# Local attention of a two-layer transformer: the first tile's norms in front of the last stage's end, inverse norms in front of divisions, queries and keys turned next to each other

## The reference

```python
x = x + band_attention(layernorm(x), ctx, ctx)       # |i - j| <= 128
y = layernorm(x)
for l in range(2):
    h = shift_token(y)                               # the upper half of the columns comes from the row before
    q, k, v = split(h @ wqkv[l])                     # 8 heads of 64
    q, k = l2norm(q) * qs[l], l2norm(k) * ks[l]      # divided by the norm of each head's 64 elements
    q, k = rotary_xpos(q, k)                         # q*cos*scale + rotate_half(q)*sin*scale; k with 1/scale
    o = local_attention(q, k, v)                     # i - 256 <= j <= i, softmax
    y = y + o @ wo[l]
    h = layernorm(shift_token(y)) * g[l] + b[l]
    a, gate = split(h @ w1[l] + b1[l])
    y = y + (a * gelu(gate)) @ w2[l] + b2[l]
return x + y
```

## Time and profile before

| | |
|---|---|
| median of three runs | 3010.24 us |
| the profiled execution: its own time / its span | 3010.82 us / 3008.8 us |
| TensorE busy | 2960.5 us, 98% of the span |
| VectorE, ScalarE, GpSimd busy | 54%, 41%, 38% |
| mean granted TensorE clock | 0.996 |
| DMA | 63 GB/s mean |

### The profile page before, as it was taken

How to read it: one execution, slowest core, us unless ns; L and a number is a source line. 1 busy time by engine, 2 the same in 40 slices (tenths; PEclk the granted TensorE clock), 3 DMA queues, 4 the chain that set the end, 5 groups by cost and what they waited for, 6 DMA issues and landing times. The chain is left out here.

```text
span 3008.8 us, 44260 instructions
## 1 busy us (share of the span) xinstructions
PE 2960.5 (98%) x17040; PEld 2418.5 (80%) x17040; DVE 1613.9 (54%) x3359; ACT 1236.6 (41%) x2497; POOL 1138.1 (38%) x1202
## 2 busy tenths in 40 slices
PE   7999999999999999999999999999999999999999
PEld 6887888888878888888887888888878888888887
DVE  6975667766764333333324667776675333433331
ACT  5874555555564111111123655555565211111111
POOL 6756556655641101111103655665561111211111
PEclk9999999999999999999999999999999999999999
DMA  7651111111042111001122111111124111111110
GB/s 238 209 177 60 43 47 43 57 43 54 29 121 63 40 45 45 31 21 39 45 85 69 32 43 50 47 50 43 54 62 128 58 45 31 53 55 52 47 53 29
DMA packets 144181, 190.52 MB, mean 63 GB/s; under 512 B 21334, under 2 KB 75098, under 8 KB 143972
## 3 DMA queue, kind: packets, MB, share of 16 engines
q1 hardware_dynamic: 143972, 187.70, 19.6%
HBM read 132.44 MB, written 52.46 MB: 61 GB/s over the span
## 5 line engine op out<-in xcount | busy, mean ns | idle before, releaser
L991 PE MATMUL quad<-fhT_f,w_h_f 128*128 128x512 f32 (+1 forms) x1392 | 551.0, 396 | 1.5 <-ACT w_h_f L1055 1.5
L993 PE MATMUL quad<-fhT_f,w_l_f 128*128 128x512 f32 (+1 forms) x1392 | 544.9, 391 | 0.0
L992 PE MATMUL quad<-fhT_f,w_h_f 128*128 128x512 f32 (+1 forms) x1392 | 543.4, 390 | 0.0
L1650 DVE SCALAR_TENSOR_TENSOR u_f<-quad,bias_f,gate_f_raw 128x512 f32<-128x512 f32 (+1 forms) x174 | 130.4, 749 | 696.3 <-PE quad L993 613.4
L1719 POOL TENSOR_SCALAR stats<-stats 128x1 f32<-128x1 f32 x64 | 43.5, 680 | 1021.5 <-DVE stats L1625 1020.9
L1807 POOL TENSOR_TENSOR turned_qk<-with_cos,with_sin 128x256 f32<-128x256 f32 x256 | 188.7, 758 | 452.3 <-DVE with_cos L1534 360.6
L1210 ACT ACTIVATE lprob<-lprob,small 128x384 f32<-128x384 f32 (+2 forms) x512 | 288.5, 565 | 160.5 <-DVE small L1509 160.5
L1313 ACT ACTIVATE gate_f_raw<-quad,bias_f 128x512 f32<-128x512 f32 (+1 forms) x174 | 119.5, 687 | 507.0 <-PE quad L993 507.0
L1055 ACT ACTIVATE uT_f<-u_f 128x512 fp32r<-128x512 f32 (+2 forms) x176 | 117.3, 666 | 511.1 <-DVE u_f L1650 511.1
L761 PE MATMUL bank_pair<-wqkv_h,hT 128*128 128x512 f32 x992 | 320.2, 404 | 1.2 <-DVE with_sin L1534 1.2
L993 PEld LDWEIGHTS quad<-fhT_f,w_l_f 128*128 128x128 f32 (+1 forms) x1392 | 256.8, 184 | 63.0
(11 more groups left out here) (223 smaller groups left out, 6034.4 us busy)
## 6 DMA issues: line engine op xcount, KB each, us to landing
s_in<-stream SPq DMA_DIRECT2D x128, 128.0 KB, 2.7
s_res<-stream SPq DMA_DIRECT2D x64, 256.0 KB, 2.9
stream<-a_out SPq DMA_DIRECT2D x64, 256.0 KB, 2.0
w_h_f_raw<-in_L_ffn_w SPq DMA_DIRECT2D x60, 256.0 KB, 5.1
h_in_f<-stream SPq DMA_DIRECT2D x112, 128.0 KB, 2.5
res_f<-stream SPq DMA_DIRECT2D x47, 256.0 KB, 3.4
x_in<-in_x SPq DMA_DIRECT2D x32, 256.0 KB, 2.8
ctx_in<-in_ctx SPq DMA_DIRECT2D x32, 256.0 KB, 2.8
```

The costliest lines, as they stand in the source:

```text
L991: e.matmul(bank[0:n, :], high, hT[:, 0, c, :], start=c == 0, stop=False)
L992: e.matmul(bank[0:n, :], high, hT[:, 1, c, :], start=False, stop=False)
L993: ins = e.matmul(bank[0:n, :], low, hT[:, 0, c, :], start=False, stop=c == KC - 1)
L1650: e.scalar_tensor_tensor(out=Fm.u[q % 2][0:n, :], in0=up_bank(2 * (g * HC + j) + 1)[0:n, :], scalar=Fm.bias1[0:n, 0, j:j + 1], in1=Fm.gate ...
```

## The change

Four things change in the local attention, the first two in its start, the others in each step.

- For layer 0 the square, the sum of squares, the scaling of the tables and the inverse norm of tile 0 stand in the band's step `TILES + 4`, before the band's last additions. For layer 1 they stay at the start of `attend(1)`, but the sum of squares stands before the multiplications by the tables, and the inverse norm before the rotation. The rotation of tile 0's keys goes from GpSimd to VectorE (`rotate_first_keys`). TensorE's second step projects 12 matmuls, turns the rows of tile 2, projects 12, and puts the turning of queries and keys between the three pieces of the value projection.
- In layer 1 a dummy exponential loads ScalarE's function table early, and the splitting of `wo` starts half a step to a step later, with its four subtractions in one step in place of two and two.
- In every step GpSimd's `inverse_norm` stands before its `divide(t, 1)`.
- In every step TensorE's `turn_q` stands directly before `turn_k`, after the second half of `project_out`, no longer between its halves.

The diff, cut to its core (places where a function only moved are left out):

```diff
+    def rotated_by_gpsimd(l, t, part):
+        return 4 * (l * TILES + t) + 2 * (part + 1) - 2 * (l + ((t, part) > (0, 0)))
...
# TensorE, attend
                 if s == 1:
-                    project(l, 1, 12, 36)
+                    project(l, 1, 12, 24)
                     turn_h(2)
+                    project(l, 1, 24, 36)
+                    turn_q(0)
                     project(l, 1, 0, 6)
-                    turn_q(0)
-                    project(l, 1, 6, 9)
                     turn_k(0)
-                    project(l, 1, 9, 12)
+                    project(l, 1, 6, 12)
...
-                    if d and 2 <= s <= TILES:
-                        turn_q(s - 1)
                     if d and ended and s not in (TILES - 1, TILES + 1):
                         project_out(tail, 1)
                     if d and 2 <= s <= TILES:
+                        turn_q(s - 1)
                         turn_k(s - 1)
...
# ScalarE, band
+                if s == TILES + 4:
+                    square(0, 0)
# ScalarE, attend
-                    if d == 0 and rotated_tile(s) is not None:
-                        square(rotated_tile(s))
+                    if d == 0 and rotated_tile(s) is not None and (l or s):
+                        square(l, rotated_tile(s))
...
+                    if l and (s, d) == (0, 0):
+                        e.activation(small[:, 0, 0:16], half_power[:, :], ACT.Exp).then_inc(S("table"), 1)
                     if d == 0 and 1 <= s < TILES - 1:
                         split_h(l, s + 1)
+                    if l and (s, d) == (2, 0):
+                        attend_split_begin(l, 3)
+                    if l and (s, d) == (3, 0):
+                        attend_split_finish(l, 3)
...
-                    if l and (s, d) == (1, 1):
-                        attend_split_begin(l, 3)
-                    if l and (s, d) == (2, 1):
-                        attend_split_finish(l, 3)
...
# VectorE, band
+                if s == TILES + 4:
+                    norm_sum(0, 0)
                 if 0 <= s - 5 < TILES:
                     band_add_x(s - 5)
# VectorE, attend
+            def rotate_first_keys():
+                n, h2 = base, HD // 2
+                turned, cos, sin = (by_head(x[:, 1, :]) for x in (A.turned_qk, A.with_cos, A.with_sin))
+                w.wait_ge(S("with_cos"), 2 * n + 2)
+                w.wait_ge(S("with_sin"), 2 * n + 2)
+                w.wait_ge(S("k_turned"), n)
+                if l:
+                    w.wait_ge(S("f_store", 0), lap(base - GROUP, GROUP))
+                for a, b in ((0, h2), (h2, 0)):
+                    e.tensor_tensor(turned[:, :, a:a + h2], cos[:, :, a:a + h2], sin[:, :, b:b + h2],
+                                    ALU.add).then_inc(S("first_rotated"), 1)
...
                     if (s, d) == (0, 0):
                         split_h(1)
+                    if l and (s, d) == (0, 0):
+                        norm_sum(l, 0)
                     if d == 0 and rotated_tile(s) is not None:
                         rope(rotated_tile(s), 0, A.with_cos, A.rope_cos, "with_cos")
                         rope(rotated_tile(s), 0, A.with_sin, A.rope_sin, "with_sin")
-                        norm_sum(rotated_tile(s))
+                    if d == 0 and rotated_tile(s):
+                        norm_sum(l, rotated_tile(s))
...
+                    if (s, d) == (0, 0):
+                        rotate_first_keys()
...
-                        if l and (s, d) == (1 + quarter // 2, 1):
+                        if l and (s, d) == (2, 1):
                             attend_split(l, 3, quarter)
...
# GpSimd, band
+                if s == TILES + 4:
+                    scale_tables(0)
+                    inverse_norm(0, 0)
                 if 0 <= s - 5 < TILES:
                     band_offset(s - 5, 4, "x1")
# GpSimd, attend
-            scale_tables()
+            if l:
+                scale_tables(l)
             wait_phase()
             for s in range(TILES + 3):
                 t = s - 2
                 live, rotating = 0 <= t < TILES, rotated_tile(s)
+                if l and s == 0:
+                    inverse_norm(l, 0)
                 if rotating is not None:
                     rotate(rotating, 0)
+                if rotating:
+                    inverse_norm(l, rotating)
                 if live:
                     divide(t, 1)
                 if rotating is not None:
-                    inverse_norm(rotating)
                     scale_rotated(rotating, 0)
-                    rotate(rotating, 1)
+                    if rotating:
+                        rotate(rotating, 1)
                     scale_rotated(rotating, 1)
```

67 lines of the change are left out of this document (38 added, 29 removed).

## The result

The changed kernel takes 2994.18 us (median of four runs, 2991.28 to 2995.27) against 3010.27 us; the ratio is 0.9947, 95% interval 0.9932 to 0.9962. The profiled execution took 2994.37 us, 16.45 us less than that of before.

A forecast was written before the change was run, and what follows sets the result against it. TensorE, busy 2960.5 of 3008.8 us, bounds the kernel; only its idle and lower-clock time can be saved. 7.5 + 0.2 + 1.0 + 2.8 + 0.1 + 0.6 + 0.6 - 0.9 = 11.9 us gives 2998.3 us, range 2995.0 to 3002.0.

The forecast's parts named there:

- Layer 0's first tile, 7.5: Start of layer 0's attention: first scores at 242.9 instead of 250.38, 7.5 us gained, of which 4.8 is TensorE's wait.
- Layer 1's first tile, 1.0: Start of layer 1's attention: first scores at 1635.1 instead of 1636.06, a gain of 1.0 us.
- what follows, 2.8 and 0.1: Layer 1's next tile gains 2.8 us as table load and `wo` copy move; moved work one step later counts +0.1.
- Eight in a row at 0.109 apiece and one such step cost 0.01 less: 0.6 us in all: Queries turned next to keys in 58 steps: joined transposes save 0.01 us each, 0.6 in all, ends 0 and 5.2.
- a sign of being wrong: All steady steps: the forecast is wrong if they change length; same-kind steps were to stay as long to 0.02 us.
- The wait of 0.46 at 464.43 ... so I count 0: TensorE's wait on GpSimd's last power of that step: inverse norm gains 0, ends -0.2 and +0.5 us per layer.
- So I take 0.3: Inverse norm before the division: queries and keys done 0.3 us earlier, 0.2 where the division is short, ends 0.1 and 0.88.
- 842.73: Place in each layer where keys are late by 0.5 us between starts; the earlier inverse norm gains 0.3 per layer.
- Step 18, -0.9: Step 18 of each layer: keys' low part comes 0.93 us later, scores 0.46 later, a loss of 0.9 for two layers.
- GpSimd's later divisions all stay hidden: Every step: the division goes 2.5 to 3.0 us later but stays within its slack, the last of each layer by 0.2.
- Rival 3: More gained from GpSimd's earlier norm and from joined transposes saving more than 0.01: 2994 to 2996.5 us; chance 0.12.
- GpSimd's 0.88: Steady steps: upper end of how much earlier queries and keys are done, GpSimd's 0.99 us idle less one hand-over.

## Why the prediction was wrong, step by step

**Layer 0's first tile, 7.5: right** (7.49). Queries were turned at 238.16, forecast 239.0, first scores at 242.04, forecast 242.9; all of it 0.84 early, as the band ended early by that much. The norms' place alone is 6.3 of it. VectorE's key addition, which the prediction worked into the chain, gives nothing in this layer.

**Layer 1's first tile, 1.0, and what follows, 2.8 and 0.1: right** (1.08, and 3.28 for steps 2 and 3). Putting the split and the table load back costs 3.1.

**"Eight in a row at 0.109 apiece and one such step cost 0.01 less: 0.6 us in all": the term that was mis-sized.** It measures 2.5 us with step 18 left out. As written the sum does not come out (8 x 0.109 + 0.09 is 0.96, more than the 0.90 of two groups); measured, four transposes take 0.355 and eight 0.798, so the 0.01 for transposes and first matmul is close to right. The step's working took the rest of the matmuls behind the transposes at 0.23. The means were 0.226 to 0.234 for them against 0.227 in a long run, a difference smaller than the two decimals that were used, and it is what all but 0.002 us of the 0.048 a step comes from. The upper end, 5.2, held the truth; the own range of the forecast did not carry it. The prediction had named this as a sign of being wrong: steady steps did change length, by 0.06.

**"The wait of 0.46 at 464.43 ... so I count 0": wrong in its premise** (1.05 in two layers by the inverse norm, shown from both sides). It said VectorE holds up the rotation by 0.44 whenever it comes, and took that to swallow the earlier start. It does not: the rotation began 0.52 earlier and took 1.41, the operation behind it lost 0.32, and the last power came 0.67 earlier.

**"So I take 0.3" for the inverse norm: too little.** In step 12 the queries are scaled 0.53 and the keys 0.66 earlier; layer 0's step 2 gained 0.41, not 0.2, and lost 0.69 when the norm went back. At 842.73 the gain was 0.32 a layer, as forecast.

**Step 18, -0.9: right** (-0.74), at the keys' low part as told, with 0.36 of wait. That GpSimd's later divisions all stay hidden held too: TensorE has no new wait for them.

Together: the forecast with 2.5 for 0.6 and 1.05 for 0 is 2995.3 us, within 1.2 of the median. That the time fell 0.8 us outside the range may itself be chance, since runs of one kernel spread by 2 to 6 us; that the two terms were too small is not, since the steps repeat.

Rival 3 was right that 464.43 gives another 0.5 per layer and that joined transposes save more than 0.01, and its range holds the median. It was wrong in the rest: GpSimd's 0.88 did not come in full, and 842.73 gave 0.32 per layer and not 0.5. It had a chance of 0.12; its parts were weighed as one event, though the trace spoke for each by itself.

## What to carry to other kernels

A term that repeats in every step must be read to the nanosecond, from means over a long run and behind a switch, before it is rounded: a few ns on some ten matmuls a step were worth more here (2.3 us over the steady steps) than a wait of 0.5 us in each layer. A hold-up between two engines belongs to the moment at which both run; move one of them and place the other's operations anew, and do not let a hold-up swallow a gain without working out where it ends. Where fp32 transposes stand in several groups among the matmuls, try joining those whose banks are free, keep the matmuls that cover a copy, and leave the one step apart in which the engine behind has no room.

## What was not expected of the hardware

- Matmuls of 512 columns behind a group of 128-column transposes start 226 to 234 ns apart in the places two to six, after a first distance of 317, and 227 ns in a long run behind that. Why is not shown.
- GpSimd's tensor_scalar on 16 columns takes 0.28 us behind the division and 0.99 beside VectorE's division of two operands in SBUF; over all tiles its mean is 0.845 in the changed kernel against 0.282 before, that of the power behind it 3.06 against 2.93:

```profile
L1785 POOL TENSOR_TENSOR norm<-norm,half_power 128x16 f32<-128x16 f32 x64 | 196.0, 3063 | 5.3
...
L1784 POOL TENSOR_SCALAR norm<-norm 128x16 f32<-128x16 f32 x64 | 54.1, 845 | 36.0 <-DVE norm L1468 35.2
```

- In the band, whose TensorE work is the same in all these kernels, the granted clock between 50 and 60 us is 1.00 in three profiles and 0.66 to 0.83 in eleven, and the stage is 3.9 us longer in the mean with the fall.
